# Batch 1's scores move to PSUM banks 4 to 7, ahead of the second pair's projections

## The reference

```python
qp = layernorm(x) @ Wq.T;  k, v = split(ctx @ Wkv_expand.T)        # 16 heads of 16
scores = einsum('bhqd,bhkd->bhqk', qh, kh) / sqrt(16);  causal mask
x = x + (softmax(scores) @ vh) @ Wout.T
x = x + moe(layernorm(x))      # 8 experts, top 2, LoRA on gate_up and down
```

## Time and profile before

| | us |
|---|---|
| median of three runs | 164.71 |
| the profiled execution | 166.08 |
| its span | 164.4 |
| TensorE busy in the span | 151.3 (92%) |
| VectorE busy | 102.4 (62%) |
| ScalarE busy | 81.7 (50%) |
| GpSimd busy | 55.9 (34%) |

### The profile page before, as it was taken

The page is one execution under the profiler, slowest core; times in us unless marked ns, Lnnn a source line. Parts: engine busy times, 40 slices in busy tenths (PEclk is TensorE's granted clock), DMA queues, the critical chain, the costliest instruction groups (busy, mean ns, idle before and its releaser), DMA issues.

```text
span 164.4 us, 3766 instructions
## 1 busy us (share of the span) xinstructions
PE 151.3 (92%) x1470; PEld 120.3 (73%) x1481; DVE 102.4 (62%) x218; ACT 81.7 (50%) x165; POOL 55.9 (34%) x95
## 2 busy tenths in 40 slices
PE   0498999899999999999999998999999999999991
PEld 0265776676787677778878886888888888888991
DVE  2656757686866674865378825874696348744443
ACT  1355477554674767766657442663563222222230
POOL 5270742245548675676863223351000000000000
PEclk9999999999999999999999999999999999999998
DMA  4999743000000000000000039500000873000003
GB/s 148 278 266 206 203 136 131 6 4 4 4 4 4 4 2 4 2 4 2 4 0 0 4 58 252 206 4 2 0 0 12 220 281 133 0 0 0 4 0 128
DMA packets 13041, 11.18 MB, mean 68 GB/s; under 512 B 6456, under 2 KB 10448, under 8 KB 13024
## 3 DMA queue, kind: packets, MB, share of 16 engines
q1 hardware_dynamic: 9584, 7.14, 16.5%
q0 software_dynamic: 544, 2.10, 4.2%
q10 hardware_dynamic: 2896, 1.70, 4.0%
HBM read 9.79 MB, written 1.08 MB: 66 GB/s over the span
## 4 chain that ended last, share of the span: by engine, by line
PE 80%; DVE 11%; issue 3%; DMA 2%; ACT 1%; POOL 1%; DVEq 0%; ACTq 0%
PE bank L808 39%; PE bank L1097 11%; PE bank L918 8%; PE bank L904 4%; PE bank L1034 4%; PE bank L925 3%; DVE m_sb L601 3%; DMA x_sb<-in_x 2%; PE bank L983 2%; PE bank L1015 1%; PE bank L889 1%; PE bank L994 1%; PE bank L855 1%; PE bank L837 1%; DVE up_w L594 1%
## 5 line engine op out<-in xcount | busy, mean ns | idle before, releaser
L601 DVE TENSOR_REDUCE m_sb<-bank 128x4 f32<-128x512 f32 x32 | 20.4, 684 | 11.0 <-PE bank L918 11.0
L396 ACT ACTIVATE probsT<-bank 128x512 f32<-128x512 f32 x32 | 17.9, 590 | 17.3 <-PE bank L925 17.3
L808 PE MATMUL bank<-xT_hi,up_hi 128*128 128x512 f32 x64 | 26.0, 407 | 0.0
L300 POOL TENSOR_SCALAR_AFFINE_SELECT probsT<-probsT 128x512 f32<-128x512 f32 x32 | 19.7, 634 | 17.0 <-ACT probsT L396 17.0
L323 ACT ACTIVATE h_hi<-h_f 128x512 fp32r<-128x512 f32 x16 | 10.1, 632 | 30.7 <-PE bank L1097 21.8
L808 PE MATMUL bank<-xT_hi,up_lo 128*128 128x512 f32 x64 | 25.3, 395 | 0.0
L808 PE MATMUL bank<-xT_lo,up_hi 128*128 128x512 f32 x64 | 25.3, 395 | 0.0
L1097 PE MATMUL bank<-dn_hi,h_hi 128*128 128x256 f32 x64 | 18.3, 285 | 0.8 <-issue 0.7
L684 DVE TENSOR_TENSOR h_lo<-h_f,h_hi 128x512 fp32r<-128x512 f32 x16 | 12.5, 779 | 10.3 <-ACT h_hi L323 10.3
L925 PE MATMUL bank<-q_f,k_f 32*128 32x128 f32 x256 | 18.6, 283 | 0.0
L1097 PE MATMUL bank<-dn_hi,h_lo 128*128 128x256 f32 x64 | 17.9, 279 | 0.0
(11 more groups left out here) (138 smaller groups left out, 284.7 us busy)
## 6 DMA issues: line engine op xcount, KB each, us to landing
probsT<-weights SPq DMA_DIRECT2D x16, 256.0 KB, 5.8
x_sb<-in_x SPq DMA_DIRECT2D x4, 256.0 KB, 4.9
up_w<-in_L_ffn_gate_up_proj ACTq DMA_DIRECT2D x1, 1024.0 KB, 11.2
up_w<-in_L_ffn_gate_up_proj POOLq DMA_DIRECT2D x1, 1024.0 KB, 8.0
dn_w<-in_L_ffn_down_proj POOLq DMA_DIRECT2D x1, 1024.0 KB, 6.3
out<-x_sb SPq DMA_DIRECT2D x4, 256.0 KB, 2.2
ctx_sb<-in_ctx ACTq DMA_DIRECT2D x2, 128.0 KB, 5.9
wq_raw<-in_L_xattn_Wq ACTq DMA_DIRECT2D x1, 256.0 KB, 6.6
```

What stands on the lines that cost most here:

```text
L300: pool.affine_select(out=ch, in_=ch, compare_op=ALU.is_ge, fill=0.0, base=0, pattern=[[0, 4], [1, P]], channel_multiplier=-1).then_inc(S_( ...
L396: act.activation(probsT[:, b % 2, 4 * j:4 * j + 4, :].rearrange("p h n -> p (h n)"), bank[2 + j % 2][:, :], ACT.Exp).then_inc(S_("exp_done ...
L601: dve.reduce_max(m_sb[:, b % 2, :].rearrange("p (u j t) -> p j u t", u=2, t=2)[:, c], S_BANK(b, c)[:, :].rearrange("p (u t n) -> p u t n", ...
L808: last = pe.matmul(out_, a, m, start=start and i == 0, stop=stop and i == len(pairs) - 1, **kw)
```

## The change

Batch 1's scores get banks 4 to 7 and follow those of batch 0. Pair 1's projections come after them, into banks 0 to 3: key halves in 0 and 1, query halves in 2 and 3. The transposed maxima of batch 0 now lie in the upper half of bank 3, so that the second query half of pair 1 is projected only after mT_copy(0). On VectorE eight maxima follow one another, and VectorE gets the copies of the second query half and of the first LoRA tile, which ScalarE had. ScalarE copies the first key half ahead of mT_copy(0) and the rest behind it.

```diff
-        K_BANK = lambda p, t: bank[(4, 6)[t] if p == NP - 1 else 4 + t]
-        Q_BANK = lambda p, t: bank[(4, 6)[t] if p == NP - 1 else 6 + t]
+        K_BANK = lambda p, t: bank[(4, 6)[t] if p == NP - 1 else t if p == 1 else 4 + t]
+        Q_BANK = lambda p, t: bank[(4, 6)[t] if p == NP - 1 else 2 + t if p == 1 else 6 + t]
-        S_BANK = lambda b, j: bank[j if b < 2 else j % 2]
-        M_BANK = lambda b: bank[6][0:NH, PN:PN + P]
+        S_BANK = lambda b, j: bank[4 * b + j if b < 2 else j % 2]
+        M_BANK = lambda b: bank[6 if b else 3][0:NH, PN:PN + P]
...
@@ scalar @@
+            k_copy(1, 0)
+            mT_copy(0)
+            k_copy(1, 1)
             q_copy(1, 0)
-            q_copy(1, 1)
-            mT_copy(0)
-            k_copy(1, 0)
-            k_copy(1, 1)
             input_copy(2)
             context_copy(2)
             values(0)
-            act.wait_ge(S_("lora_T"), 1)
-            copy(loraBT[:, 0, :, :].rearrange("p a n -> p (a n)"), bank[4][:, :], "upB_ready", LORA)
@@ vector @@
+            q_copy(1)
             context_dup(2)
+            dve.wait_ge(S_("lora_T"), 1)
+            dve.tensor_scalar(loraBT[:, 0, :, :].rearrange("p a n -> p (a n)"), bank[4][:, :], LORA, None, ALU.mult)\
+                .then_inc(S_("upB_ready"), 1)
@@ tensor: x_T(2), context_T(2) @@
+                if p == 2:
+                    pe.wait_ge(S_("max_done"), NC + 1)      # context_T(2): NC + 2
@@ tensor: k_proj(1) @@
-                    pe.wait_ge(S_("xT_ready"), 2)
+                    pe.wait_ge(S_("max_done"), 2)
@@ tensor: q_proj(p, ts) @@
                 if p == 1:
-                    pe.wait_ge(S_("q_copied_0"), 2)
-                    pe.wait_ge(S_("q_copied_1"), 2)
+                    pe.wait_ge(S_("max_done"), 3 + ts[0])
+                    if ts[0]:
+                        pe.wait_ge(S_("mT_copied"), 1)
@@ tensor: v_proj(0) @@
-                    pe.wait_ge(S_("q_copied_0"), 4)
-                    pe.wait_ge(S_("q_copied_1"), 4)
-                    pe.wait_ge(S_("mT_copied"), 1)
+                    pe.wait_ge(S_("max_done"), 2 * NC)
@@ tensor: the masks of scores(1) @@
-                        if s:
-                            pe.wait_ge(S_("max_done"), n - 3 if s == 1 else n - 1)
+                        if s == 1 and j < 2:
+                            pe.wait_ge(S_(("xT_ready", "cT_lo")[j]), 2)
+                        if s > 1:
+                            pe.wait_ge(S_("max_done"), n - 1)
@@ tensor @@
             scores(0, (0, 1, 2, 3), None, ())
-            q_proj(1)
+            scores(1, (0, 1, 2, 3), None, ())
             k_proj(1)
+            q_proj(1, (0,))
             max_T(0)
-            scores(1, (0, 1, 2, 3), None, ())
+            q_proj(1, (1,))
             x_T(2)
```

More of the change, by code:

```diff
@@ L820, in context_T @@
                 pe.wait_ge(ld[f"ctx{p // 2}"], 16)
-                if p in (1, 2):
-                    pe.wait_ge(S_("k_copied_1"), 2 * p)
+                if p == 1:
+                    pe.wait_ge(S_("k_copied_1"), 2)
+                if p == 2:
+                    pe.wait_ge(S_("max_done"), NC + 2)
                 if p == 3:
@@ L830, in x_T @@
                 pe.wait_ge(S_("xhat_ready"), 2 * (p + 1))
-                if p in (1, 2):
-                    pe.wait_ge(S_("k_copied_0"), 2 * p)
+                if p == 1:
+                    pe.wait_ge(S_("k_copied_0"), 2)
+                if p == 2:
+                    pe.wait_ge(S_("max_done"), NC + 1)
                 if p == 3:
@@ L856, in k_proj, with q_proj @@
                               start=True, stop=True).then_inc(S_(f"k_proj_{t}"), 1)
-            def q_proj(p):
+            def q_proj(p, ts=(0, 1)):
                 pe.wait_ge(S_("xT_ready"), p + 1)
@@ L871, in q_proj @@
                     pe.wait_ge(S_("o_T_copied"), 1)
-                for t in range(2):
+                for t in ts:
                     products(Q_BANK(p, t)[:, 0:PN], [(wq_d[:, ic, t * P:(t + 1) * P], xT[:, p % 2, ic, :]) for ic in range(HC)],
@@ L931, in max_T @@
                 pe.wait_ge(S_("max_done"), NC * (b + 1))
-                if b == 0:
-                    pe.wait_ge(S_("q_copied_0"), 4)
                 if b == 1:
```

## The result

The change costs time: 167.38 us (median of four runs, 166.97 to 167.61) against 165.06 us (four runs of the kernel before, 163.92 to 165.47). The ratio is 1.0135, with a 95% interval of 1.0089 to 1.0182, so about 2.2 us more. Run again beside other variants it was 1.0132 [1.0098, 1.0166]. I had forecast 165.9 us and a range up to 167.2; the sign of the shift and the place of the new waits were right, the size wasn't.

A forecast was written before the change was run, and what follows sets the result against it. TensorE, busy 92% of the span, was taken to bound the kernel. A 1.15 us delay at the loop's first scores, containing the 0.44 us hole, added to the 164.71 us median gave 165.86, rounded 165.9 us; range 164.4 to 167.2.

The forecast's parts named there:

- The hole: TensorE idle before pair 1's second query half, waiting for ScalarE's copy of batch 0's transposed maxima: 0.44 us.
- The next thing late: Load of batch 0's maxima, issued 0.97 us later, amid the down_proj load; the loop's first scores wait for it.
- the step from the load's issue at 21.67 to its release at 26.7: Load of batch 0's maxima, both parts moved into the down_proj flood, releasing the loop's first scores 1.15 us later.
- some 0.6 us: Time from the maxima's second part's packets, 25.0 or a little before, to the release at 25.57, added again.
- The term: Delay of the loop's first scores by the maxima's load: 1.15 us, containing the 0.44 us hole.
- the slower rival: Maxima's load comes last in the flood, the loop starts at 27.6: delay 2.0 us, 166.7 us in all; chance 0.19.
- The rule of taking turns: DMA engines alternate between queues packet by packet, so the small load waits about a packet per engine: the lower bound, 0.44 us.

The follow-up runs named there:

- the edit that frees the load: The kernel before with GpSimd's down_proj load issued behind batch 0's four masks: ratio 0.9997 to the kernel before.
- the variant with bank 2: The changed kernel with batch 0's transposed maxima in bank 2 and no wait for their copy ahead of the second query half: ratio 1.0104.

## Why the prediction was wrong

**Right, by the runs.** TensorE was the bound and had nothing to gain (its idle in the stretch was 0.10 us; before, the edit that frees the load gains 0.0). The new order costs what its rows say: scores, key projection and half query projection end at 21.04, where I had 21.07, or 20.83 with the early start; the 0.2 are an idle of 0.16 ahead of the masks and 0.10 more for the half projection. The hole was forecast at 0.44 and is 0.45. The eight maxima took 4.88 us, forecast 4.96. Nothing moved to VectorE or taken from ScalarE set an end. The next thing late was the maxima's load, held by the down_proj load.

**Wrong: the step from the load's issue at 21.67 to its release at 26.7.** The prediction put "the first to where the second was, the second (22.4) to where the router's loads were", with packets at 26.0 to 26.2, and added "some 0.6 us". The term was 1.15 us (26.7 - 25.57 is 1.13) and measured 2.17. Two things in it failed.
- The parts don't keep their places in a row. Before, the second part was moved in the middle of the big load; after, neither was. The second of before was issued some 0.6 us behind the big load's issue, and the first of after 0.85. In all five executions where the maxima's first part was issued some 0.8 us or more behind the big load from GpSimd, both parts went at its end; at 0.46 (the variant with bank 2) the first still went in the middle. The sum should have taken the end of the big load as the time of both parts' packets.
- "Some 0.6 us" from the last packet to the release came from one part in the middle of the big load. With both parts and the router's loads together at its end, the last part landed at 27.47, when nearly all packets were moved by 26.5: about 1 us. What makes it longer stays open; without the router's loads it may be up to 0.35 less, which one trace can't tell from scatter.

So it went the way of the slower rival, the load last in the flood, at 27.6 with a price of 2.0 us; it had a chance of 0.19. What I held against it, that SyncE keeps the maxima ahead of the router's loads, is true of the issue, and didn't bring the load in sooner. The nearest row to a part issued at 22.4 was indeed the router's load issued at 22.50; but I read the window in which its packets were moved and not when it landed, and no row of the small load's own landing stood against it. The range was short by 0.2 us, because its top was this rival and half a microsecond of scatter above a median of 164.71, and the kernel before is at 165.06 over four runs.

**The rule of taking turns.** For 3.5 us the runs show no packet of the small loads, while 216 of the big one's were moved. With the small load on ScalarE's queue, its 24 packets came behind 25 too. The Trainium skill, "DMA: Bandwidth & Descriptors", section "Queues, rings and completion order", has the engines take turns between queues packet by packet; by that alone the load would have been in time. The trace disagrees for this load, whether the big one came from GpSimd or from ScalarE (no small packet between 21.21 and 23).

That the load on ScalarE's own queue took 5.04 us, against 5.27 on SyncE's, agrees with another statement. The Trainium skill, "Trainium Kernel Development and Optimization", section "Key Constraints", says that the queues of all issuing engines run on the same 16 DMA engines and that several of them only save issue time.

## What to carry to other kernels

When a change delays a small load that an engine waits for, look at what big load starts next to it: here the difference was worth 2.2 us, whether the small load was issued 0.16 us ahead of the big one or 0.85 us behind it. A small load that came in time may have had hardly any slack (some 0.03 us here); test it by delaying it alone. A big load that isn't needed for a long time belongs behind the small ones with a deadline; moving it cost no time here (0.9997, with an interval of 0.9966 to 1.0029). And filling the holes of an engine that isn't the bound (2.3 us on VectorE) gave nothing here (1.0007 with both of the change's own waits removed); it may help only where the order of the bound itself uses it.

## What the runs showed of the hardware

- The maxima's second part, a small DMA issued 1.2 to 2.0 us behind a 1 MB load from GpSimd, took 4.9 to 5.3 us from issue to landing (5.27, 5.20, 5.12, 5.04, 4.94 and 4.85 in six executions). In the quiet the packets of both parts were through within 2.5 us of the first issue.
- Lateness can cost more than itself: 0.97 us later, in the order of before, cost 1.98 us, and the same lateness without the big load cost 0.01 (8.05 against 8.04).
- Most small packets went at the big load's end, whether the big load was on GpSimd's queue or on ScalarE's. Some did pass among the big load's: 12 before (24 to 25), 12 in the bank 2 variant, 17 of the router's in the one where ScalarE issues the maxima's load. What decides isn't shown.
- A releaser named in a row is no proof of a wait: the row at 25.57 named the load, with 0.42 us, and the same 0.42 stand there as "issue" when the load's packets are through 1.9 us before.
